# Decoder layer on one core: GpSimd's gate and transfers, one bank's products, two quarter copies and two query blocks change places

## The reference, cut to what matters

```
x = layernorm(x + hyena(x));  x = layernorm(x + cross_attention(x, ctx));  x = layernorm(x + bit_ffn(x))
# hyena, batch 4, L = 1024, D = 256, ORDER = 2:
res = depthwise_conv3(u @ w_in.T + b_in)      # taps left, middle, right
x0, x1, v = res.reshape(B, 3, D, L)
for n in range(2):
    y = irfft(rfft(v, 2L) * rfft(h[n], 2L))[..., :L]
    v = y * x[n]                              # the gate
return v.T @ w_out.T + b_out
```

## Time and profile before

| | |
|---|---|
| time, median of 3 runs | 756.21 us (755.85 to 756.58) |
| the profiled execution | 755.24 us, span 753.4 us |
| busy in the span | PE 90%, DVE 85%, ACT 49%, POOL 49% |
| mean granted clock of TensorE | 0.980 |
| filter stage | from 0 to about 473 us of the span |
| one full batch (GpSimd's gate of batch 1 to that of batch 2) | 199.27 to 300.33 us |

### The profile page before, as it was taken

The page is one execution under the profiler, slowest core; times in us unless marked ns, Lnnn a source line. Parts: engine busy times, 40 slices in busy tenths (PEclk is TensorE's granted clock), DMA queues, the critical chain, the costliest instruction groups (busy, mean ns, idle before and its releaser), DMA issues. The chain is left out here.

```text
span 753.4 us, 12524 instructions
## 1 busy us (share of the span) xinstructions
PE 681.7 (90%) x4414; PEld 498.3 (66%) x4414; DVE 638.9 (85%) x1237; ACT 372.0 (49%) x689; POOL 371.6 (49%) x510
## 2 busy tenths in 40 slices
PE   6899999978999888999787999998999999999995
PEld 2488766857748766568566786656777776665664
DVE  3997787799979899898999677557899996999997
ACT  6342255211173501665013623577666667877785
POOL 0844424746145652258531561580582322877885
PEclk9999999989999999999899899999999999999999
DMA  8440047312043380233731074810000000001012
GB/s 305 125 92 1 0 115 165 57 20 37 1 83 74 96 139 0 46 67 83 138 73 57 10 190 108 292 45 2 1 2 3 2 2 2 2 10 48 30 56 86
DMA packets 34970, 50.18 MB, mean 67 GB/s; under 512 B 4729, under 2 KB 29050, under 8 KB 34652
## 3 DMA queue, kind: packets, MB, share of 16 engines
q0 software_dynamic: 7680, 16.77, 13.4%
q1 hardware_dynamic: 26364, 31.82, 13.0%
q10 hardware_dynamic: 864, 0.79, 0.4%
HBM read 29.46 MB, written 7.34 MB: 49 GB/s over the span
## 5 line engine op out<-in xcount | busy, mean ns | idle before, releaser
L659 ACT ACTIVATE yb<-banks 128x256 f32<-128x256 f32 x64 | 24.4, 386 | 215.1 <-PE banks L410 155.3
L401 PE MATMUL banks<-inv_m,spec_y 128*128 128x256 f32 x384 | 87.9, 381 | 8.7 <-POOL spec_y L776 8.7
L358 PE MATMUL banks<-z_cplx,fwd_m 128*128 128x256 f32 x240 | 76.1, 400 | 21.2 <-DVE z_cplx L951 15.8
L433 PE MATMUL banks<-xt_in,w_in 128*128 128x512 f32 x192 | 86.4, 606 | 1.8 <-DMA w_in<-in_w_in_t 1.8
L401 PEld LDWEIGHTS banks<-inv_m,spec_y 128*128 128x128 f32 x384 | 72.2, 190 | 21.8 <-POOL spec_y L776 12.4
L775 POOL TENSOR_TENSOR spec_y<-prod 128x256 f32<-128x256 f32 x64 | 49.5, 773 | 57.7 <-DVE prod L1004 56.6
L359 PE MATMUL banks<-z_cplx,fwd_m 128*128 128x256 f32 x240 | 74.3, 392 | 0.0
L433 PEld LDWEIGHTS banks<-xt_in,w_in 128*128 128x128 f32 x192 | 37.1, 195 | 47.2 <-issue 43.6
L358 PEld LDWEIGHTS banks<-z_cplx,fwd_m 128*128 128x128 f32 x240 | 47.0, 200 | 31.4 <-DVE z_cplx L951 17.0
L1003 DVE TENSOR_TENSOR prod<-banks,spec_h 128x512 f32<-128x512 f32 x64 | 43.9, 687 | 16.6 <-POOL spec_y L776 9.5
L359 PEld LDWEIGHTS banks<-z_cplx,fwd_m 128*128 128x128 f32 x240 | 47.8, 199 | 7.2
(11 more groups left out here) (280 smaller groups left out, 1691.5 us busy)
## 6 DMA issues: line engine op xcount, KB each, us to landing
x_tok<-in_x SPq DMA_DIRECT2D x8, 512.0 KB, 4.4
x_tok<-in_b_out POOLq DMA_DIRECT2D x8, 512.0 KB, 12.8
v_t<-left POOLq DMA_DIRECT2D x8, 511.5 KB, 5.5
x_t<-left POOLq DMA_DIRECT2D x8, 511.5 KB, 4.7
xt_in<-in_x_t SPq DMA_DIRECT2D x3, 1024.0 KB, 6.2
x_scratch<-x_tok SPq DMA_DIRECT2D x6, 512.0 KB, 4.0
x<-x_scratch SPq DMA_DIRECT2D x6, 512.0 KB, 9.3
out<-x SPq DMA_DIRECT2D x6, 512.0 KB, 2.9
```

Source lines behind the costliest of these rows:

```text
L358: mm(o, fwd_m[:, at + 2 * half + odd, :], zz[:, 0, :], start=True, stop=False)
L401: last = mm(bank[:, odd * 2 * P:(odd + 1) * 2 * P], spec_y[:, j + odd, part * D + h * P:part * D + (h + 1) * P], inv_m[:, o:o + 2 * P], st ...
L433: last = mm(proj_pair(b, t)[:, c * 512:(c + 1) * 512], w_in[:, k, TILES[t] * P:(TILES[t] + 1) * P], xt_in[:, k, c * 512:(c + 1) * 512], st ...
```

## The change

- POOL: in the batches but the last, the two `add_left` of tiles 4 and 5 go from between the additions of banks 3/4 and 4/5 of transform u + 1 to behind them all. `add_bias` goes ahead of `gate_first(u + 1)`, and `gate_first(u + 1)` goes from ahead of the additions of transform u + 2 to between its banks 3 and 4.
- DVE: the addition and the subtraction of bank 7 of every transform go from POOL to DVE, right behind that bank's products. `level_one` of (u + 1, h = 0) then waits for all 8 banks at its start, where it waited for 7 there and for the eighth a little later.
- ACT and DVE, tile 3 of the next batch: the first two quarter copies stand ahead of its left tap, and on DVE the first quarter difference stands ahead of its right tap.
- Last batch: queries 1 goes ahead of the turn of x0_t, queries 2 ahead of fwd, rows 3 between the two halves of inv; ACT's copies and the waits move with them.

```diff
 PE, last batch
                     queries(0, IB[0:2], [...])
-                    pe.wait_ge(rows_evac, DT * 2)
+                    queries(1, IB[2:4], [...])
                 pe.wait_ge(gated, 2 * (u + 1))
                 turn(x0_t)
                 if last_one:
-                    queries(1, IB[2:4], [...])
                     pe.wait_ge(query_evac, DT)
                     turn_rows(2, IB[0:2])
+                    queries(2, IB[2:4], [(query_evac, DT + t + 1) for t in range(DT)])
...
-                    pe.wait_ge(query_evac, DT * 2)
+                    pe.wait_ge(query_evac, DT * 3)
                     pe.wait_ge(rows_evac, DT * 3)
                 inv(u + 1, 0)
+                if last_one:
+                    pe.wait_ge(prod_done, 8 * 2 * B)
+                    turn_rows(3, FB[2:4])
...
-            pe.wait_ge(prod_done, 8 * 2 * B)
-            turn_rows(3, FB[2:4])
-            queries(2, FB[0:2])
             pe.wait_ge(rows_evac, DT * 4)
             turn_rows(4, FB[2:4])
-            queries(3, FB[0:2], [(query_evac, DT * 2 + t + 1) for t in range(DT)])
-            pe.wait_ge(rows_evac, DT * 5)
+            queries(3, FB[0:2])
             queries(4, IB[0:2], [...])
             pe.wait_ge(query_evac, DT * 4)
+            pe.wait_ge(rows_evac, DT * 5)
             out_project(B - 1, 8 * 2 * B)
 ACT
-                    taps_from(b + 1, T_V, T_X0)
+                    taps_from(b + 1, T_V, T_X0 - 1)
+                    mid_tap_of(b + 1, T_X0 - 1)
...
-                evac_turn(u + 1)
+                evac_turn(u + 1, 0, 2)
+                if not last_one:
+                    left_tap_of(b + 1, T_X0 - 1)
+                evac_turn(u + 1, 2, 4)
 POOL
-            def add_products(u, first=False, left_of=None):
-                for j in range(BANKS):
-                    if left_of is not None and j in (4, 5):
-                        add_left(left_of, T_X0 + j - 4)
+            def add_products(u, first=False, j0=0, j1=BANKS - 1):
+                for j in range(j0, j1):
...
-                add_products(u + 1, left_of=None if last_one else b + 1)
+                add_products(u + 1)
+                if not last_one:
+                    for t in range(T_X0, T_ALL):
+                        add_left(b + 1, t)
                 if not last_one:
                     if b:
                         norm_factors(b - 1)
                     turned_real_sums(u + 2)
-                if last_one:
-                    add_bias(b)
+                add_bias(b)
+                if not last_one:
+                    add_products(u + 2, j1=4)
                 gate_first(u + 1, ...)
                 if not last_one:
-                    add_bias(b)
-                if not last_one:
-                    add_products(u + 2)
+                    add_products(u + 2, j0=4)
 DVE
                 signal(tt(r2[:, 0], x0, x2_copy, ALU.subtract))
+                if right_of is not None:
+                    right_tap(right_of, T_X0 - 1)
                 if evacuated is not None:
                     dve.wait_ge(xq_evac, evacuated + 4)
                 signal(tt(r2[:, 1], x1, x3_copy, ALU.subtract))
...
                         .then_inc(prod_done, 1)
+                    if j == BANKS - 1:
+                        dve.wait_ge(prod_done, 8 * (u + 1))
+                        tt(spec_y[:, j, 0:D], prod[:, s, 0:D], prod[:, s + 1, D:2 * D], ALU.subtract)
+                        tt(spec_y[:, j, D:2 * D], prod[:, s + 1, 0:D], prod[:, s, D:2 * D], ALU.add).then_inc(y_ready, 1)
...
                 if at:
-                    dve.wait_ge(y_ready, 8 * u + 7)
+                    dve.wait_ge(y_ready, 8 * (u + 1))
...
-                if at:
-                    dve.wait_ge(y_ready, 8 * (u + 1))
...
-                    for t in range(T_V, T_X0):
+                    for t in range(T_V, T_X0 - 1):
                         right_tap(b + 1, t)
-                turned_sums(u + 1)
+                turned_sums(u + 1, None if last_one else b + 1)
```

## The result

The changed kernel takes 759.7 us (median of 6 runs, 758.6 to 764.0), the kernel before 756.3 us (755.1 to 756.9, 6 runs beside it). The ratio is 1.006, 95% interval 1.0038 to 1.0081. It is slower: the medians lie 3.4 us apart, and by the ratio it is about 4.5. Forecast were 743.9 and a range that ended at 750. The profiled execution took 758.58 us, its span is 756.8.

The account below looks back on a forecast made before the run. DVE and handovers to it were taken to bound 75 us of a batch, PE the other 26.10. Gains of 2.6 a batch (7.9), plus 2.05 and 2.4, made 12.35 off 756.21: 743.9 us, range 741.5 to 750.

Parts of the forecast that it names:

- Bias and tokens: add_bias ahead of banks 0 to 3: batch 1's tokens come at 265.45 us, slack 0.8 us, so no cost.
- The slack of 0.8: In batch 1, bias DMA issued by 266.8 us, bank 0's product done at 267.6, so add_bias delays nothing.
- POOL stands at add_bias: Late tokens hold POOL: each us beyond 0.8 slack delays banks 0 to 3, batches 1 and 2; chance 0.03.
- the tie: Gate between banks 3 and 4 and L1029 both due at 276.76: L1029 first loses 1.0 us, gate first 2.3.
- the gate blocks L1029: Gate issues first and L1029 waits it out: 1.3 us a batch more, 3.9 in all, 747.8 us; chance 0.30.
- The argument that a third wait makes the gate later: A two-wait instruction came after 0.81 us; the gate has three waits, so L1029 was taken as first, loss 1.0.
- the forecast's 1.0: Loss in us a batch if L1029 goes first and the moved gate blocks only L1036.
- The batch's other terms: Gains in us: quarter copies 0.34, DMAs and bank 7 (u + 1) 0.84, unblocked L956 2.14, bank 7 (u + 2) 0.3.
- The clock rival: PE's clock falls in its longer wait for L1072: some 2.6 us, three times, 751.7 us; chance 0.07.
- The last batch: Moved queries fill PE's idle before the turn, 2.05 us; out_project's second part starts earlier, 2.4 more: 4.45 in all.

Follow-up runs that it names:

- e2: Changed kernel, GpSimd awaiting both token loads before it issues the first group's bias transfer: 750.27 us, ratio 0.9925 to the kernel before.
- e8: Changed kernel, next batch's input load (`xt_in`, 1 MB) held back until the tokens have landed: 757.46 us in one execution.
- e3: Kernel before, with add_bias alone moved ahead of the gate: 767.42 us, ratio 1.0147.
- e15: e1 with two TensorE waits of batches 1 to 3 (first inverse's later complex banks, out_project) filled with extra matmuls: 748.50 us, ratio 0.9896 to the kernel before.
- e5: Kernel before, with the gate alone moved between banks 3 and 4 and the bias transfers behind it: 756.23 us, ratio 0.9997.
- e11: e9 plus a third TensorE wait filled and level one's two small SBUF differences put behind the bank reads: 748.56 us, ratio 0.9904 to the kernel before.
- e14: e1 with level one's two small SBUF differences put behind the bank reads: 747.37 us, ratio 0.9873 to the kernel before.
- e16: e1 with add_bias moved behind GpSimd's last additions (banks 4 to 6): 748.80 us, ratio 0.9902 to the kernel before.
- e7: Kernel before, with only the first two quarter copies moved ahead of tile 3's left tap: 755.55 us, ratio 0.9995.
- e12: e6 with TensorE's out_project wait of batches 1 to 3 filled by repeating its first pass: 752.67 us, ratio 0.9955 to the kernel before.
- e1: Changed kernel with add_bias back behind the gate, which stays between banks 3 and 4: 749.68 us, ratio 0.992 to the kernel before.
- e6: Kernel before, with only bank 7 on VectorE and the two add_left behind the banks: 754.73 us (751.5 to 760.1), ratio 0.998.
- e4: Kernel before, with only the last batch's part of the change: 753.13 us, ratio 0.9959.
- e9: e2 with two TensorE waits of batches 1 to 3 (first inverse's later complex banks, out_project) filled with extra matmuls: 751.80 us, ratio 0.9947 to the kernel before.
- e13: Changed kernel with add_bias last on GpSimd, level one's small differences behind the bank reads and three TensorE waits filled: 746.67 us, ratio 0.9868 to the kernel before.

## Why the prediction was wrong

**The step that failed is "Bias and tokens".** Its times have to be read from the gate of the batch, since batch 1 began at 199.27 before and begins at 198.20 now. The step had the tokens at 265.45, 66.2 us after the gate. SP issued the second load 61.8 us after it; by the 3.8 us of before they would have been there at 65.6, so the issue was forecast well. What it got wrong is the landing. It moved the transfer of group 0's bias ahead of the second load without asking what that transfer does to the load: it costed the 1.28 us that the DMA occupies on GpSimd, and not the 12.6 us for which it runs. The load then took 11.1 us, and the tokens came at 271.1, 72.9 us after the gate and 6.7 later than the step said (6.4 in batch 2). In e2, without the transfer beside them, the wait for them ends 66.1 us after the gate. e2 and e8 tell the cause from its rival: without GpSimd's own transfer beside it the load takes 3.7 and 3.9 us, with the 1 MB load held back it still takes 9.6 (10.5 in batch 2). e3 shows it without the rest of the change. The slack of 0.8 held: bank 0's product was done 68.6 us after the gate (at 266.76), where the step had 68.3.

The rival "POOL stands at add_bias" had the place, the batches and the rule right, with a chance of 0.03: each us beyond the slack of 0.8 counts in batches 1 and 2. By its rule 6.7 and 6.4 late cost 5.9 and 5.6 us; against e15's trace it is 105.57 - 99.73 = 5.8 and 105.23 - 99.71 = 5.5, 11.4 together. Its evidence against, that the load had landed in about 4 us each time, came from a kernel in which the adding transfer was issued only at 264.20, when the load of 262.47 was nearly in.

The Trainium skill (DMA: Bandwidth & Descriptors, "Queues, rings and completion order") says that each DMA engine takes the queues that it has work for in turn, a packet at a time, so transfers of two queues share the engines. The traces agree in so far as the load is slowed by a transfer of the other queue, but 3.7 to 11.1 us is three times, and 9.6 with the 1 MB load held back is 2.6 times. That is more than sharing with one other transfer of the same 512 KB would make if both got equal parts; no run here shows what makes the adding transfer so heavy.

**The gate took the other side of the tie.** The step took 1.0 and kept 2.3. L1029, now L1038, took 2.43 in place of 0.28: the gate issued at 278.33, 0.11 us ahead of it, and VectorE lost 2.15 us. That is the rival "the gate blocks L1029", 0.30, 747.8. With it the gate's move is worth 2.14 - 2.15 (2.3 was the bound), nothing, and e5 measured 0.9997, with its gate at 276.51 again 0.11 ahead of the small sum. The argument that a third wait makes the gate later did not hold here: from the start of the addition ahead of it (277.64) to the gate are 0.69 us, less than the 0.81 that I took from an instruction of another kind. e11 and e14 reach the forecast's 1.0 by the code's order, not by a tie: with the bank reads first the loss is 1.2, and e14's batch 2 takes 98.69 us where 98.4 was forecast.

The Trainium skill (SBUF — State Buffer, "Who interferes with whom") says that a VectorE instruction with at most one input in SBUF, outside the 2-port modes, does not contend with GpSimd. e14's reads at 0.41 beside the gate, each with one input in a bank and one in SBUF, agree.

**The batch's other terms were right together.** With the rival's 2.3 the sum of a batch is 0.34 + 0.84 + 2.14 - 2.3 + 0.3 = 1.32; e15's batches are 101.06 - 99.73 = 1.33 shorter. e16 shows the same without filled waits (1.36 in each of batches 1 and 2). 756.21 - 3 x 1.32 - 4.45 = 747.8; e15 took 748.5, e16 748.8. That the sum of a batch comes out to 0.01 us is luck: term by term less is shown. e7's 0.34 is inside the noise, e12 took 0.45% (3.4 us, with a filled wait; forecast for this part 3 x 1.14), and batch 0 gained 1.9 us where 1.3 would be its share.

**The clock rival was partly real.** Forecast was a wait of 2.4 us for L1072's successor, L1081; it is 2.15. In the profiled runs of e1 and e6 the matmuls behind it took 1.7 us more each of the five times that it came; at 295.12 in the changed kernel and at 289.22 in e16 they did not. Elsewhere (e2, e16, the changed kernel) it was the wait ahead of the two later inverse banks, 2.55 us, behind which 16 matmuls took 5.40 in place of 4.13, which the next wait absorbed. So the fall comes and goes from batch to batch within one execution, and costs 1.7 us where it counts, not the 2.6 forecast; in e6 it goes with the spread. Another part of the spread lies ahead of it: the first gate came at 95.83 in the changed kernel, at 97.45 in e1 and at 95.78 in e15, which do the same work up to there. I had given the two outcomes of the clock one price for all batches; it is a chance for each.

**The last batch was right**, a little large: 4.45 forecast, 3.9 measured in the changed kernel, 3.1 for its own edits alone (e4). The 16 transposes take 1.97 us (3.65 in the earlier trace rows) behind 0.28 of waiting, VectorE's wait of 2.08 has become 1.63, and the second part of the last `out_project` starts behind L1081 as said. TensorE in the changed kernel's last batch:

```profile
414.49 7.10 PE L523 MATMUL banks<-spec_h,left 128*128 128x512 f32 x16
...
421.87 1.97 PE L424 MATMUL banks<-ident,x_t 128*128 128x128 f32 x16 [0.28 <-DVE x_t L1081]
...
467.64 1.89 PE L453 MATMUL banks<-w_out,v_t 128*128 128x256 f32 x8
470.40 5.45 PE L453 MATMUL banks<-w_out,v_t 128*128 128x256 f32 x24 [0.88 <-DVE v_t L1081]
```

The ledger: 743.9, plus 3.9 for the gate, plus 11.4 for the tokens is 759.2, against 759.7. The 11.4 is taken from the trace that it explains (the rival's rule gives 11.5), and small misses offset each other in the sum (batch 0 gained 0.6 more than its share, the first gate came 0.8 late, the end gained 0.5 less), so that it closes to 0.5 us is partly luck. One bound of the range was added loosely: 743.9 less 1.0 and less 1.0 is 741.9, not 741.5; nothing rests on it. What stays open: why one adding transfer slows a load so much; whether the instruction packets delay the stores in e9; and why e13's combined edits give less than their parts.

## What to carry to other kernels

Moving a DMA's issue moves the whole transfer: ask what is in flight while it runs, and whether what its queue waits for next is among that. An instruction list with a wait in front of hot work should first gather all its waits and then issue, not alternate; in e2 that alone was worth 9 us. When edits gather several short waits of TensorE into one, the clock may fall behind it. Matmuls whose result is overwritten kept the clock up in every wait filled here, and the times lay closer together (8.6 us in e6, 2.2 in e12); a gain in the median is only likely, and none came where tokens set the pace. And compare batches in the traces before medians: 1.0 us a batch for the order stands out there, while the medians of e1 and e14 have intervals that touch.

## What the runs showed of the hardware

- A load of 512 KB took 3.7 to 4.5 us, and 9.6 to 11.1 while GpSimd's adding transfer of 512 KB (medians of 10.5 to 13.9 us) ran; the load of 1 MB 5.7 to 6.2, and 13.2.
- Behind a wait of 2.15 us the matmuls ran at the full clock in some batches and partly at the lower level in others (5.45 or 7.13 us for 24), in the same kernel; behind waits of 0.42 to 0.43 and 0.85 to 0.90 at the same place the 24 took 5.45 in every trace.
- GpSimd's multiplication of 128x1024 (2.35 us) lets VectorE's reads of banks through at 0.41 us and holds its first SBUF-only instruction to the end, even one of 0.28 us.
